# Attention in halves on one core: key and value steps one place forward, exponentials ahead of an eviction, angles in other halves

## What is computed

```python
x = x + xattn(layernorm(x), ctx, ctx, ...)
x = x + attn(layernorm(x), ...)
x = x + ffn(layernorm(x), ...)
...
def quantum_circuit(v):
    return jnp.cumprod(jnp.cos(v), axis=-1)
...
score = jnp.einsum('bhqd,bhkd->bhqk', q, k) * SCALE
attn = jax.nn.softmax(score, axis=-1)
out = jnp.einsum('bhqk,bhkd->bhqd', attn, v)
...
xh = x.reshape(B, T, H, dk)
attn_out = quantum_circuit(xh).reshape(B, T, C)
x1 = layer_norm(x + attn_out, gamma1, beta1)
q = quantum_circuit(x1[..., :nq])
h = jnp.einsum('btq,fq->btf', q, w1) + b1
ffn_out = jnp.einsum('btf,cf->btc', jax.nn.relu(h), w2) + b2
```

## Time and profile before

| | |
|---|---|
| median of three runs | 1748.42 us |
| profiled execution, its own time | 1745.66 us |
| its span, first to last instruction | 1743.9 us |
| mean granted clock of TensorE | 0.978 of full speed |
| busy: PE, VectorE, ScalarE, GpSimd | 95%, 82%, 70%, 54% |

### The profile page before, as it was taken

One profiled execution on the slowest core, in us unless ns is written; L12 is line 12 of the kernel. 1 busy time (PEld: TensorE's weight loads), 2 busy tenths in 40 slices (PEclk: granted clock), 3 DMA queues, 4 the chain that ended last, 5 costly groups with the idle time before them and its releaser, 6 DMA issues. The chain is left out here.

```text
span 1743.9 us, 59225 instructions
## 1 busy us (share of the span) xinstructions
PE 1651.4 (95%) x24340; PEld 1352.1 (78%) x24340; DVE 1430.6 (82%) x3316; ACT 1218.2 (70%) x3297; POOL 948.6 (54%) x1427
## 2 busy tenths in 40 slices
PE   7999999999999999999999999996698899999998
PEld 4777777777777777777777777775476899999998
DVE  6698988989889898898888989889775776766657
ACT  3677877778777787777877788777555265656552
POOL 5355556555565555655556555553411448888850
PEclk9999999999999999999999999997797999999999
DMA  5011111211112111121111211111102356666632
GB/s 176 22 64 45 64 48 42 67 45 64 48 42 67 45 64 48 42 67 45 63 49 42 67 45 63 49 45 60 62 25 85 116 180 220 224 223 223 221 122 103
DMA packets 43439, 147.89 MB, mean 85 GB/s; under 512 B 5680, under 2 KB 25008, under 8 KB 39712
## 3 DMA queue, kind: packets, MB, share of 16 engines
q1 hardware_dynamic: 38416, 130.72, 21.9%
q0 software_dynamic: 4752, 13.38, 2.4%
HBM read 129.79 MB, written 14.16 MB: 83 GB/s over the span
## 5 line engine op out<-in xcount | busy, mean ns | idle before, releaser
L498 ACT ACTIVATE a_probs<-a_probs,a_bias 128x401 f32<-128x401 f32 x1024 | 632.0, 622 | 2.1
L728 DVE STREAM_TRANSPOSE a_pT<-a_probs 128x1664 f32<-128x1664 f32 x256 | 488.0, 1906 | 93.5 <-ACT a_probs L498 64.8
L713 DVE TENSOR_SCALAR_CACHE_REDUCE a_probs<-a_pss 128x401 f32<-128x401 f32 x1024 | 527.0, 570 | 25.6 <-PE a_pss L965 8.5
L965 PE MATMUL a_pss<-a_keys,a_qown 32*32 32x401 f32 x8192 | 253.2, 507 | 24.7 <-issue 23.4
L315 POOL TENSOR_TENSOR a_clo<-a_raw,a_chi 128x416 fp32r<-128x416 f32 x240 | 251.5, 1079 | 0.0
L994 PEld LDWEIGHTS a_pso<-a_pT,a_v 128*32 128x32 f32 x6656 | 182.2, 111 | 43.6 <-issue 40.5
L338 POOL TENSOR_SCALAR a_ex<-a_probs,a_marks 128x4 f32<-128x4 f32 x256 | 75.5, 295 | 253.2 <-ACT a_probs L498 252.9
L994 PE MATMUL a_pso<-a_pT,a_v 128*32 128x128 f32 x6656 | 199.7, 277 | 2.5 <-ACT a_op L513 2.1
L1661 PE MATMUL e_psg<-e_xh,e_guh 128*128 128x256 f32 x660 | 189.5, 287 | 5.5 <-DVE e_hl L1407 4.0
L498 ACT ACTIVATION_READ_ACCUMULATOR a_probs<-a_probs,a_bias 128x1 f32 x1024 | 194.4, 190 | 0.0
L1662 PE MATMUL e_psg<-e_xl,e_guh 128*128 128x256 f32 x660 | 186.7, 283 | 0.0
(11 more groups left out here) (253 smaller groups left out, 4249.9 us busy)
## 6 DMA issues: line engine op xcount, KB each, us to landing
a_raw<-in_ctxT SPq DMA_DIRECT2D x60, 832.0 KB, 4.4
f_gur<-in_wgu SPq DMA_DIRECT2D x24, 1408.0 KB, 6.5
f_dr<-in_wd SPq DMA_DIRECT2D x24, 768.0 KB, 4.7
e_big<-ys_scr SPq DMA_DIRECT2D x8, 512.0 KB, 7.3
a_probs<-in_ctxT SPq DMA_DIRECT2D x2, 1664.0 KB, 9.3
a_x<-in_x SPq DMA_DIRECT2D x16, 128.0 KB, 4.3
rows_scr<-f_a SPq DMA_DIRECT2D x8, 256.0 KB, 2.3
rows_scr<-f_a SPq DMA_DIRECT2D x4, 512.0 KB, 3.5
```

Of the source, the lines that this page charges most:

```text
L498: nc.scalar.activation(z, z, ACT.Exp, bias=bias[:, h % 2, at_bias:at_bias + 1], scale=-1.0, accum_out=esum[:, h % 2, j, 2 * e + r:2 * e + ...
L713: nc.vector.tensor_scalar(probs[:, at % RING, j, 0:KG], ps_s[:, j, 0:KG], -SCALE, None, ALU.mult, ALU.min, accum_out=nmax[:, h % 2, at_max ...
L728: nc.vector.transpose(pT[:, turned_slot(h, i)].rearrange("p j k -> p (j k)"), probs[:, at % RING].rearrange("p j k -> p (j k)")).then_inc( ...
L965: mm = nc.tensor.matmul(ps_s[32 * g:32 * g + 32, j, 0:KG], q_own[32 * j:32 * j + 32, n % 2, m, e, 32 * r:32 * r + 32], keys[32 * j:32 * j ...
```

## The change

- `steps_in`: each half takes its steps one place further: even halves 2 to 9, odd halves 10 to 14 and steps 0 and 1 of the batch after; the first period takes one step more.
- PE: `spread` stands ahead of the whole quarter 3, not behind its first step.
- ACT: at the end of a half the first pair of exponentials comes after one step's copy of quarter 2, the second pair after the rest of quarter 2, ahead of the first copy of quarter 3 and of the copy of the output.
- Angles: in halves 61 and 62, not 62 and 63. Turns 3 to 6 leave the last half and stand among the steps of `DVE_ORDER`, and the last inverse comes first there. The table load and the first two cosines come ahead of the last copy of the output. On GpSimd the split of w1 comes after the first power, and three memsets ahead of the last gather.
- Two tensors are allocated earlier in SBUF (`ffn_row`, `tri_sb`), which moves what lies behind them.

```diff
     if h < 0:
-        plan = [[(0, 4), (0, 5), (0, 6)], [(0, 7), (0, 8), (0, 9)], [(0, 10), (0, 11), (0, 12)], [(0, 13), (0, 14), (1, 0)]]
+        plan = [[(0, 4), (0, 5), (0, 6)], [(0, 7), (0, 8), (0, 9)], [(0, 10), (0, 11), (0, 12)], [(0, 13), (0, 14), (1, 0), (1, 1)]]
     elif h % 2 == 0:
-        plan = [[(n + 1, 1)], [(n + 1, 2), (n + 1, 3)], [(n + 1, 4), (n + 1, 5)], [(n + 1, 6), (n + 1, 7), (n + 1, 8)]]
+        plan = [[(n + 1, 2)], [(n + 1, 3), (n + 1, 4)], [(n + 1, 5), (n + 1, 6)], [(n + 1, 7), (n + 1, 8), (n + 1, 9)]]
     else:
-        plan = [[], [(n + 1, 9), (n + 1, 10), (n + 1, 11)], [(n + 1, 12), (n + 1, 13)], [(n + 1, 14), (n + 2, 0)]]
+        plan = [[], [(n + 1, 10), (n + 1, 11)], [(n + 1, 12), (n + 1, 13)], [(n + 1, 14), (n + 2, 0), (n + 2, 1)]]
...
         DVE_ORDER = order(
-            "rows.0 inverse.0 scan.0 residual.0 scan.1 scale1.0 residual.1 q_angles.0 circuit.0 scan.2 residual.2 last_rows.0 scale1.1 scale1.2 affine.0 "
+            "inverse.0 rows.0 scan.0 residual.0 turns.3 scan.1 scale1.0 q_angles.0 residual.1 turns.4 circuit.0 turns.5 scan.2 turns.6 residual.2 last_rows.0 scale1.1 scale1.2 affine.0 "
...
         ACT_ORDER = order(
-            "out.0 table.0 cos.0 cos.1 cos.2 cos.3 centre_q.0 centre1.0 cos.4 q_cos.0 copy_q.0 relu.0 relu.1 relu.2 relu.3 relu.4 relu.5 relu.6 "
+            "table.0 cos.0 cos.1 out.0 cos.2 centre_q.0 centre1.0 q_cos.0 cos.3 copy_q.0 cos.4 relu.0 relu.1 relu.2 relu.3 relu.4 relu.5 relu.6 "
...
         POOL_ORDER = order(
-            "pow1.0 pow1.1 pow1.2 by.0 pow1.3 pow1.4 pow2.0 pow1.5 pow3.0 pow2.1 pow2.2 pow3.1 pow3.2 pow2.3 pow3.3 pow2.4 pow3.4 pow2.5 pow3.5 ")
+            "pow1.0 w1.0 pow1.1 pow1.2 by.0 pow1.3 pow1.4 pow2.0 pow1.5 pow3.0 pow2.1 pow2.2 pow3.1 pow3.2 pow2.3 pow3.3 pow2.4 pow3.4 pow2.5 pow3.5 ")
...
-        ANGLES_IN = {(NH - 2, 1): (0, 1), (NH - 2, 2): (2,), (NH - 2, 3): (3,), (NH - 1, 1): (4,), (NH - 1, 2): (5,)}
-        TURNS_IN = {0: (0,), 1: (1,), 2: (2,), 3: (3, 4, 5, 6)}
+        ANGLES_IN = {(NH - 3, 1): (0,), (NH - 3, 2): (1, 2), (NH - 3, 3): (3,), (NH - 2, 1): (4,), (NH - 2, 2): (5,)}
+        TURNS_IN = {0: (0,), 1: (1,), 2: (2,), 3: ()}
...
-                copy_steps(steps[2])
-
+                copy_steps(steps[2][:1])
                 if h + 1 < NH:
                     copy_bias(h + 1)
                     exponentials(h + 1, 0, FORMER)
+                copy_steps(steps[2][1:])
+                if h + 1 < NH:
+                    exponentials(h + 1, 0, LATTER)
                 copy_steps(steps[3][:1])
                 if h > 0:
                     copy_out(h - 1)
-                if h + 1 < NH:
-                    exponentials(h + 1, 0, LATTER)
                 copy_steps(steps[3][1:])
...
-                for z in steps[3][:1]:
-                    step(*z)
                 if h > 0:
                     spread(h - 1)
-                for z in steps[3][1:]:
+                for z in steps[3]:
                     step(*z)
```

More of the change, by code:

```diff
@@ L116, in attention_and_circuit @@
             b1_sb, wr_sb, rb_sb = sbc("f_b1", [P, FC]), sbc("f_wr", [P, NC, E]), sbc("f_rb", [P, E])
+            ffn_row, tri_sb = sbc("f_frow", [P, D]), sbc("f_tri", [P, P])
             u, heads, t, c, a = (sbc(f"f_{n}", [P, NT, D]) for n in ("u", "hd", "t", "c", "a"))
             w1_raw = a[0:3 * HD, 8:12, :].rearrange("p a b -> p (a b)")
-            ffn_row, w1_sb = sbc("f_frow", [P, D]), sbc("f_w1", [P, FF], F32R)
+            w1_sb = sbc("f_w1", [P, FF], F32R)
             qx, qn, qc, q_heads, qs = (sbc(f"f_{n}", [P, NT, HD]) for n in ("qx", "qn", "qc", "qhd", "qs"))
@@ L122, in attention_and_circuit @@
             gu_raw, d_raw = sbc("f_gur", [P, 2, NC, 2 * EI]), sbc("f_dr", [P, 2, EC, D])
-            tri_sb, cnt_sb, lg = sbc("f_tri", [P, P]), sbc("f_cnt", [P, P + 1 + SLOTS + E]), sbc("f_logits", [P, NT, E])
+            cnt_sb, lg = sbc("f_cnt", [P, P + 1 + SLOTS + E]), sbc("f_logits", [P, NT, E])
             hT, xT = sbc("f_hT", [P, 2, FC, 512]), sbc("f_xT", [P, 4, 2 * NC, P])
@@ L468, in _ @@
             nc.gpsimd.memset(w1_sb[:].bitcast(F32), 0.0).then_inc(zeroed, 1)
-            gather(NH - 1)
             nc.gpsimd.memset(q_heads[:], 0.0).then_inc(zeroed, 1)
@@ L472, in _, with split_w1 @@
             nc.gpsimd.memset(qT[:].bitcast(F32), 0.0).then_inc(zeroed, 1)
[L473 to L478, removed]
+            gather(NH - 1)
+            def split_w1():
+                pool.wait_ge(loaded, 16 * 7)
+                pool.wait_ge(zeroed, W1_ZERO)
+                nc.gpsimd.tensor_copy(w1_sb[0:3 * HD, :], w1_raw).then_inc(w1_split, 1)
+                pool.wait_ge(w1_split, 1)
+                nc.gpsimd.tensor_tensor(out=w1_sb[2 * HD:3 * HD, :], in0=w1_raw[2 * HD:, :], in1=w1_sb[2 * HD:3 * HD, :].bitcast(F32), op=ALU.subtract).then_inc(w1_split, 1)
+                pool.wait_ge(w1_split, 2)
             pool.wait_ge(expo_set, 2)
             for stage, g in POOL_ORDER:
+                if stage == "w1":
+                    split_w1()
+                    continue
                 if stage == "by":
@@ L860, in _ @@
                     residual(NT - 1)
+                elif stage == "turns":
+                    round_turns(g)
+                    leave_turns(g)
                 elif stage == "round":
```

## The result

The changed kernel takes 1733.6 us (median of four runs, 1732.5 to 1735.9), the one before 1748.6 (1747.9 to 1750.0): a ratio of 0.992 (0.991 to 0.993). It is faster by 15 us, about half of the 29 forecast; 1733.6 lies just outside the stated range (1708 to 1733).

A forecast was written before the change was run, and what follows sets the result against it. PE's order of work and its one wait per block were taken as the bound; attention -26 and tail -3 gave -29 on a profiled 1745.7 us, 1716.7, plus 2.8 to the median: 1719, range 1709 to 1728, stated 1708 to 1733.

The forecast's parts named there:

- The even half: Attention, PE: the wait of 0.73 goes and one interruption (0.18) is saved, 19.34 to 18.43 us.
- What is late next: Odd halves: PE reaches `spread_max` before DVE's reduction ends; waits 0.18, with a projection 0.32; halves become 16.59 and 17.59.
- K12 goes, -1.17: Odd half, PE: key step 12 leaves its start, saving 1.17 us, the price of a key step inside a run.
- Attention's sum: Even halves -28.2, plain odd halves 0.0, odd halves with a projection +2.0: -26 us.
- the forecast's bound without waits at `spread_max`: Attention's favourable bound: with no PE wait for DVE's reduction in odd halves, -32 us instead of -26.
- half comes back: Rival: odd halves become DVE's, `spread_max` or score quads behind it wait 0.4 more per block; attention -14, 1731; chance 0.12.
- The exponentials ahead at nothing: ACT, end of a half: two exponentials moved ahead give DVE its transposition earlier, but PE doesn't wait for it; costed at nothing.
- DVE was the bound: Rival: the 64.8 us DVE's transpositions wait for ACT come back through the exponentials ahead; 1684; chance 0.04.
- Slower: Rival: exponentials ahead of a copy keep a PSUM bank occupied and PE waits before a step; 1795; chance 0.04.
- doesn't do what it says: Rival: a key step's copy ends late behind ACT's exponentials, S0 waits as before, only interruptions are saved; 1742; chance 0.06.
- The tail: After attention: earlier scan, power and `turn_q`, partly given back on ACT and DVE; -3 us, bounds +1 and -7.
- The split's price: Tail: the weight split on POOL slows a DVE operation beside it (2.65 against 0.68); the 2 us stay in the chain.

The follow-up runs named there:

- the attention part alone: Kernel before with only the change's attention edits (steps one place forward, exponentials ahead, spread ahead of its quarter), angles and tail as before: 1735.6 us, ratio 0.992.
- the profile at 1.00: Two further reciprocals per half on VectorE, added to the changed kernel with one key step given back and three even-half steps in one run: 1703.2 us.
- the kernel it was built from: Changed kernel with one key step given back to the odd half and three steps in one run in even halves: 1708.5 us, ratio 0.977.

## Why the prediction was half right

Half of the forecast gain came, and nearly all that is missing is lost in the odd halves.

- **The even half: right.** The wait of 0.73 is gone and the half is 18.39 (forecast 18.43).
- **The odd half: wrong, and this is the step that failed.** "What is late next" asked only about `spread_max`, behind the reduction, and gave 0.18. The reduction was no problem (over at 704.04, `spread_max` at 704.55). What was late is the quad before it: S0 needs the evictions of the quad ahead, whose last ends 8.16 after the opening quad in both kernels (the chain starts from PE's weighting, which follows that quad at once). Priced there, "K12 goes, -1.17" becomes 9.02 - 9.63 = -0.61 (end of S0 after the opening quad, after and before). With the +1.03 measured behind S0 (forecast +0.99) the half is +0.42 (forecast 0.00), with a projection +0.70 (forecast +0.14), since there the spare was only 0.3. I had treated a score quad as a fixed 0.9 and asked for waits only where the profile prints them.
- **Attention's sum.** Over the whole part 31 x (18.39 - 19.34) + 16 x 0.42 + 14 x 0.70 = -12.9, against the -26 forecast. In the trace it is -10.9 from half 0 to half 60, with 30 even halves; half 0 is in that with 18.05 for 16.80, half 1 with 17.01 for 17.74. That half 0 would give back the first period's extra step was wrong: by `steps_in` it has eight steps in either kernel, and half 61 is the one with a step less (five for six). And the forecast's bound without waits at `spread_max` is miscounted: odd halves at -0.18 give -28.2 - 30 x 0.18 = -33.6, not -32, which changes nothing here.
- **The rival "half comes back" comes nearest**: the odd half became VectorE's, a block lost 0.4 to 0.6 against the forecast, and 1731 is near 1733.6. But its words name `spread_max` and the score quads behind it; the quad that waited stands ahead of it, so the place was not foreseen there either. I gave it 0.12 because in the even half nothing of this showed. The evidence that would have raised it, the last eviction against the start of S0 (0.58), was one row away.
- **The exponentials ahead at nothing: right**, by the run without them. "DVE was the bound" is out with it. The rule on matmul busy time that I cited there (Trainium Kernel Development and Optimization, Best Practices, of the Trainium skill: not to judge the distance to roofline by matmul busy time) does not speak for VectorE here; what the trace shows is that PE's own busy time rose by 14.7 us while the kernel became faster.
- **"Slower" and "doesn't do what it says": out.** PE waits nowhere for the copy of a step, and S0 of the even half starts with no pause.
- **The tail: right by itself (-3.7 alone, forecast -3), its parts roughly; with the attention part it won nothing in the trace.** Behind the last transposition it is -2.7, but that transposition, which I had left where it is, came 3.1 later after half 60. The scan came 8.1 earlier (forecast some 10; ahead of it L880 took 2.15, before 0.17), the power 7.2 (7.4), `turn_q` 4.3 (6), relu 1.1 (2 to 3). The split's price stayed in the chain as said, but with other victims: L857 took 0.91 (0.16 before) and L897 1.69 (0.18), together 2.3. The second of ACT's two cosines ahead of relu waited 1.93 for the rounds of angles.
- **Not foreseen:** half 62 at the lower clock, in the profile 3.3 us longer than with the attention part alone, 2.5 longer than before. What brings it stays open.

## What to carry to other kernels

Before a step is taken out in front of a group of matmuls, look at when the engine behind it frees each bank that the group writes, and at how far ahead of the group that is: the spare, not the step's price, is what can be won. A group that waits inside itself shows as busy, so compare the mean length of the group and the distance of starts, not idle time alone. And where two halves alternate, put the steps where the other engine's chain is late: here one step moved back was worth more than the whole change.

## What was not expected of the hardware

The granted clock in the second layer, from 30 us behind the last transposition to the last `expand`, was 0.91 on average in ten of the twelve profiles here, 0.95 in one and 1.00 in one, for nearly the same instructions. Between the last transposition and the last `expand` the profile at 1.00 is 6.7 us shorter than that of the kernel it was built from, and the medians of these two kernels with equal halves differed by 5.4. So a few us between two medians here say little; the lengths of the halves, which repeat to a hundredth, say more. In half 62 of the change the clock fell from 2.4 to 1.2 GHz in a quad in which PE stood waiting for evictions, although the profile calls it busy, and the weighting behind it took 5.6 instead of 3.0 us; with twelve matmuls of work put ahead of that quad, and in the other variants without them, it did not. The Trainium skill (TensorE: Matmul & The Clock Gate, A second HAM failure mode) describes short pauses between groups of matmuls that cycle through PSUM, seen in a bf16 kernel, as a way to lose the clock. The traces don't settle whether that is it: the change's two profiles would fit, but with the attention part alone the same quad waits 1.5 with the clock at 1.00, and so do the score quads of the odd halves, which wait 0.55 to 0.83 each (from 140 to 1140 us the granted clock was 1.00). Why the change has this dip in both its profiles, and the attention part alone and the other variants have not, stays open.
